# Between two layers: splitting the five later Silus of ScalarE into two and three

## The chip, the cores and the metric

The kernel runs on one core of a Trainium2 chip. The metric is the device time of one execution in microseconds; the figure of a kernel is the median of several executions. The five engines work in parallel, each through its own instructions in program order, and meet at semaphores: PE (TensorE, with its weight loads PEld), DVE (VectorE), ACT (ScalarE), POOL (GpSimd) and SP, which only issues DMAs.

## The reference

Two layers, each of the form `x = x + s * silu(g)` with `xn = layernorm(x)`; `s` comes from an attention-like part, `g` from a mixture of experts.

```python
x = L0_attn_x                                   # (4, 1024, 256): 4096 tokens
xn = _layernorm(x, axis=-1)
s = _L0_attn_ref(xn, ...)                       # windows of 64 tokens, 16 heads
g = _silu(_L0_ffn_ref(xn, ...))                 # 32 experts, one per token
x = x + s * g
xn = _layernorm(x, axis=-1)
s = _L1_attn_ref(xn, ...)                       # Fourier spectra, cumulative sum over tokens
g = _silu(_L1_ffn_ref(xn, ...))                 # 8 experts, two per token
x = x + s * g
```

The change lies between the layers: in `x = x + s * g` of the first, and in the layernorm, the transposition and the first spectra of the second.

## The kernel before

The 4096 tokens are 32 tiles of 128 rows; `X`, `XN` and `S` in SBUF hold x, the normalized x (later the first layer's mixture output, reloaded into the same place) and s. Between the layers the work goes by eight **quarters** of four tiles, numbered q = 0 to 7, with first tile g = 4q. For each quarter there are these steps, and the name of a step stands in a plan that each engine reads in order, doing its own part of it:

- `mix_load` (SP, L2545): the mixture's output is loaded into `XN`.
- `mix_silu` (ACT, L2213): Silu in place over 128x1024.
- `mix_mul` (DVE, L1591): `S = XN * S` over 128x1024.
- `mix_sum`: `X = X + S`, on DVE for quarters 0 and 1 (L1598), on POOL for 2 to 7 (L2370); SP then stores the quarter of `X` (L2560).
- `stats` (DVE, L1355 to L1360): mean and variance of the four tiles, and variance + eps; then ACT takes the square root (L2078).
- `norm`: DVE takes the reciprocal of the root (L1365), the shift (L1367), and normalizes two of the four tiles (L1371); ACT normalizes the other two (L2223); SP stores them (L2549).
- `turn`: PE transposes the quarter (L1037), ACT copies it from PSUM to `XT1` (L2085).
- `spectrum`: one of the second layer's spectra on PE (L1048). Its copy out of PSUM, `spectrum_out` (L2069), is put off until the plan next asks for it with `need`.
- `route1`: for every two quarters, router logits on PE (L1247), copied to `route1_rows` by ACT (L2237), and later `route1_turn`, their transposition (L1076) and copy (L2242). After the last of these DVE adds the router's bias (L1698) and starts the routing of the second layer.

The plan of this part is written out by hand in `combination()` inside `schedule0`. An item that is put off with a lag of 0 (`route1_out`) comes into the plan at the next `add`; one with the lag `LATER` comes only when `need` names it.

Silu and Sqrt are in different activation tables. Where an ACTIVATE needs another table than the one loaded, an ACT_TABLE_LOAD stands ahead of it on ACT; Copy and Identity need none of their own. Such a load has the line of the instruction that it serves (L2213 for Silu, L2078 for the root).

What each engine waits for at the places in question, in the words of the code:

```python
elif what == "mix_silu":                      # ACT: only for the load of its quarter
    w.wait_ge(x_in[q], 32)
if what == "stats":                           # ACT: the root waits for DVE's variance
    w.wait_ge(ln_var, nth)
def normalize(layer, g):                      # DVE: waits for the root on ACT
    w.wait_ge(ln_root, nth)
elif what == "route1_out":                    # ACT: waits for PE's router logits
    filled_by(use["route1", g])
elif what == "mix_mul":                       # DVE: waits for the Silu
    w.wait_ge(gated0, q + 1)
```

Of the kernel before, what the change touches and what calls it, by code (L numbers as in the profile page):

```python
# [132 lines left out]
QUARTERS = NT // 4  # L133
# [17 lines left out]
class Order:  # L151
# [10 lines left out]
    def need(self, item):  # L162
        for due, _, pending in list(self.late):
            if pending == item:
                self.settle(due)

    def add(self, what, *at):
        self.settle(self.clock)
        self.plan.append((what, *at))
# [31 lines left out]
LATER = STEPS * UT  # L201
SPECTRA_AHEAD = [(ch, n) for ch in range(AHEAD) for n in (KK, VV, QQ)]


def spectrum_bank(ch, n):
    return (3 * ch + (KK, VV, QQ).index(n)) % 2


def schedule0(banks):

    order = Order(banks)
    add, need = order.add, order.need
# [52 lines left out]
    def turn(layer, g, tiles=8):  # L265
        for t in range(g, g + tiles, 2):
            order.take(("turn", layer, t // 2), (4, 5)[(t // 2) % 2])
        add("turn", layer, g)
# [16 lines left out]
    def route1(g):  # L285
        order.product("route1", g, columns=0, then=[("route1_out", 0)])

    def route1_turn(g):
        need(("route1_out", g))
        order.product("route1_turn", g, columns=0, then=[("route1_turn_out", LATER)])  # L290
# [89 lines left out]
    def spectrum(ch, n, lag):  # L380
        order.product("spectrum", ch, n, bank=spectrum_bank(ch, n), columns=0, then=[("spectrum_out", lag)])

    def combination():
        add("load_wf")
        for q in range(QUARTERS):
            add("mix_load", q)
        for q in range(3):
            add("mix_silu", q)
        add("mix_mul", 0)
        add("mix_sum", 0)  # L390
        add("stats", 1, 0)
        add("norm", 1, 0)
        turn(1, 0, 4)
        spectrum(*SPECTRA_AHEAD[0], LATER)
        for q in range(3, QUARTERS):
            add("mix_silu", q)
        add("mix_mul", 1)
        add("mix_sum", 1)
        add("mix_mul", 2)
        add("mix_sum", 2)  # L400
        add("stats", 1, 4)
        add("mix_mul", 3)
        add("mix_sum", 3)
        add("stats", 1, 8)
        for q in range(1, QUARTERS):
            g = 4 * q
            if q % 2 == 0:
                need(("route1_turn_out", g - 8))
            add("norm", 1, g)
            if q + 3 < QUARTERS:  # L410
                add("mix_mul", q + 3)
                add("mix_sum", q + 3)
            need(("spectrum_out", *SPECTRA_AHEAD[q - 1]))
            turn(1, g, 4)
            if q % 2 == 0:
                route1_turn(g - 8)
            spectrum(*SPECTRA_AHEAD[q], LATER)
            if q % 2:
                route1(g - 4)
            if q + 2 < QUARTERS:  # L420
                add("stats", 1, g + 8)
        need(("spectrum_out", *SPECTRA_AHEAD[QUARTERS - 1]))
        route1_turn(4 * QUARTERS - 8)
        need(("route1_turn_out", 4 * QUARTERS - 8))
# [28 lines left out]
    assert next(ffn, None) is None  # L453
    order.settle(order.clock + STEPS * UT)
    combination()
    order.settle(order.clock + STEPS * UT)
    return order.plan
# [2216 lines left out]
```

## Time and profile before

| | |
|---|---|
| median of 3 runs | 1121.63 us (1120.66 to 1124.16) |
| the profiled execution | 1117.8 us, span of its instructions 1115.8 us |
| PE / DVE / ACT / POOL busy in the span | 92% / 62% / 48% / 37% |
| mean granted TensorE clock | 0.968 of full speed |

The profiled execution is one more execution beside the timed ones; its times below are microseconds from the start of its span. "Busy" of an engine is the share of the span in which it worked on an instruction. The chain of waits is followed back from the last instruction, at each step to what released it. The first layer ends on PE at about 420 us, the stretch between the layers ends at about 472 us, where DVE starts the routing of the second layer, and the second layer's experts run on PE from about 534 us to the end.

### The profile page before, as it was taken

How to read it: one execution, taken by the hardware profiler on the slowest of the kernel's cores; microseconds unless marked ns; L12 is line 12 of the kernel's file. 1: busy time of each engine (PE TensorE's matmuls, PEld its weight loads, DVE VectorE, ACT ScalarE, POOL GpSimd, SP SyncE). 2: the span in 40 equal slices, each digit the busy share in tenths (PEclk: the TensorE clock that was granted, in tenths of full speed). 3: DMA queues.
4: the chain of work that ended last, by engine and by line, in shares of the span. 5: the costliest groups of instructions: out<-in, count | busy, mean ns of one | idle time of the engine just before them, and what ended most of it. 6: DMA issues, size and time to landing. Idle time of an engine off the chain costs nothing.

```text
span 1115.8 us, 16806 instructions
## 1 busy us (share of the span) xinstructions
PE 1026.7 (92%) x6152; PEld 886.4 (79%) x6152; DVE 688.6 (62%) x1490; ACT 532.2 (48%) x1102; POOL 418.1 (37%) x391
## 2 busy tenths in 40 slices
PE   3867899999999994979999999999999999999994
PEld 2655788888888873668889998988888888888884
DVE  6796777777777767687846644474676100148753
ACT  3633754555545536733454545455353222356531
POOL 1056545554455452200243322332331345432273
PEclk9988999999999996987999999999999999999998
DMA  9932245445565428525497754544344679899961
GB/s 301 283 141 86 81 124 189 153 153 180 163 193 190 126 89 275 184 95 249 103 350 260 291 204 180 203 166 156 110 168 154 241 265 343 320 336 389 392 256 55
DMA packets 120402, 228.65 MB, mean 205 GB/s; under 512 B 14939, under 2 KB 103915, under 8 KB 115329
## 3 DMA queue, kind: packets, MB, share of 16 engines
q1 hardware_dynamic: 106448, 189.31, 48.7%
q0 software_dynamic: 13872, 38.27, 10.4%
q8 instruction: 49, 0.80, 0.3%
q14 instruction: 33, 0.26, 0.1%
HBM read 166.98 MB, written 62.79 MB: 206 GB/s over the span
## 4 chain that ended last, share of the span: by engine, by line
PE 74%; DVE 12%; ACT 4%; issue 3%; DMA 3%; POOL 2%; SPq 0%; POOLq 0%; DVEq 0%; ACTq 0%
PE PS L1314 21%; PE PS L1324 20%; PE PS L1213 6%; PE PS L1048 4%; PE PS L1098 3%; PE PS L1152 3%; PE PS L1223 2%; PE PS L1179 2%; PE PS L1107 2%; POOL table L2335 2%; PE PS L1165 2%; PE PS L1190 2%; DVE stats L1355 1%; PE PS L1300 1%; PE PS L1289 1%
## 5 line engine op out<-in xcount | busy, mean ns | idle before, releaser
L2292 ACT ACTIVATE hT<-PS,WE 128x256 f32<-128x256 f32 (+1 forms) x312 | 141.0, 454 | 255.2 <-PE PS L1314 240.1
L1314 PE MATMUL PS<-xgT,WE 128*128 128x256 f32 (+1 forms) x1248 | 253.3, 361 | 2.6 <-ACT hT L2292 1.8
L1324 PE MATMUL PS<-WE,hT 128*128 128x256 f32 x1104 | 244.6, 379 | 0.0
L1314 PEld LDWEIGHTS PS<-xgT,WE 128*128 128x128 f32 x1248 | 219.4, 190 | 29.4 <-ACT hT L2292 2.5
L1324 PEld LDWEIGHTS PS<-WE,hT 128*128 128x128 f32 x1104 | 207.4, 190 | 26.9
L1951 DVE TENSOR_TENSOR y<-PS,WE 128x512 f32<-128x512 f32 (+1 forms) x38 | 24.3, 640 | 206.9 <-PE PS L1324 201.7
L2410 POOL DMA_INDIRECT result<-y,result_of x53 | 53.8, 1016 | 175.8 <-DVE y L1951 168.6
L2398 POOL DMA_INDIRECT xg<-xn_dram,token_of x71 | 74.3, 1046 | 90.7 <-DVE result_of L1867 68.7
L1048 PE MATMUL PS<-XT,Wf 128*128 128x256 f32 x384 | 93.4, 399 | 3.3 <-ACT Z L2069 3.3
L1048 PEld LDWEIGHTS PS<-XT,Wf 128*128 128x128 f32 x384 | 75.1, 201 | 15.3 <-ACT Z L2069 4.9
L2351 POOL TENSOR_TENSOR prob<-prob,row_sum 128x512 f32<-128x512 f32 x56 | 58.6, 1046 | 59.8 <-DVE row_sum L1531 59.1
L1213 PE MATMUL PS<-rowsT,wgu 128*128 128x160 f32 x512 | 75.6, 301 | 0.0
L2344 POOL TENSOR_TENSOR sc<-sc,sc_max 128x512 f32<-128x512 f32 x56 | 58.5, 1045 | 42.7 <-DVE sc_max L1519 42.3
L1213 PEld LDWEIGHTS PS<-rowsT,wgu 128*128 128x128 f32 x512 | 71.9, 190 | 2.3 <-issue 1.4
L1098 PE MATMUL PS<-XT,qkv_w 128*128 128x256 f32 x256 | 64.6, 397 | 0.0
L1529 DVE TENSOR_REDUCE row_sum<-prob 128x8 f32<-128x512 f32 x64 | 43.5, 680 | 29.0 <-ACT prob L2160 26.0
L2386 POOL TENSOR_TENSOR MAG<-SQ 128x768 f32<-128x768 f32 x13 | 25.0, 1926 | 93.2 <-ACT SQ L2259 93.2
L1037 PE MATMUL PS<-const,XN 128*128 128x128 f32 x128 | 26.0, 353 | 35.9 <-DVE XN L1371 34.0
L2362 POOL DMA_INDIRECT mixed_dram<-y,row_token x40 | 39.7, 993 | 47.4 <-DVE y L1585 43.0
L2170 ACT ACTIVATE PT<-PS 128x512 f32<-128x512 f32 x64 | 38.3, 599 | 39.7 <-PE PS L1165 37.5
L1098 PEld LDWEIGHTS PS<-XT,qkv_w 128*128 128x128 f32 x256 | 48.0, 197 | 8.3 <-issue 1.1
L2335 POOL DMA_INDIRECT table<-XN,slot_put x32 | 32.4, 1012 | 58.0 <-DVE slot_put L1459 42.5
(280 smaller groups left out, 1711.9 us busy)
## 6 DMA issues: line engine op xcount, KB each, us to landing
WE<-in_experts SPq DMA_DIRECT2D x39, 2180.0 KB
wgu<-in_w_gate SPq DMA_DIRECT2D x32, 256.0 KB
wgu<-in_w_up SPq DMA_DIRECT2D x32, 256.0 KB
wdn<-in_w_down SPq DMA_DIRECT2D x32, 256.0 KB
result<-zeros SPq DMA_DIRECT2D x16, 512.0 KB
xs<-late_dram SPq DMA_DIRECT2D x16, 512.0 KB, 12.9
both<-result SPq DMA_DIRECT2D x16, 512.0 KB
table<-zeros POOLq DMA_DIRECT2D x1, 5160.0 KB, 31.2
```

Of the source, the lines that this page charges most:

```text
L1048: m = e.matmul(PS[:, u.bank, part * CH:(part + 1) * CH], Wf[:, n, k, part * P:(part + 1) * P], XT1[:, ch, k, :], start=k == 0, stop=k == K ...
L1098: m = e.matmul(PS[:, u.bank, c * UT:(c + 1) * UT], qkv_w[:, k, col:col + P], XT0[:, unit, k, :], start=k == 0, stop=k == KD - 1)
L1213: m = e.matmul(PS[:, u.bank + f, n * CAP:(n + 1) * CAP], wgu0[:, ex % 2, n, k, f * P:(f + 1) * P], rowsT[:, grp % 2, k, j * CAP:(j + 1) * ...
L1314: m = e.matmul(PS[:, FIRST_H_BANK + nth % HR, 0:rows], W1[n % WR][:, k, c * P:(c + 1) * P], xgT[:, n % 2, k, 0:rows], start=k == 0, stop=k ...
L1324: m = e.matmul(PS[:, u.bank, j * D:(j + 1) * D], hT[:, n % 2, c, j * P:(j + 1) * P], W2[n % WR][:, c, :], start=c == 0, stop=c == KF - 1)
L1529: e.tensor_reduce(row_sum[:, s % RR, :], prob[:, s % PR0, :, :], AX.X, ALU.add).then_inc(row_sum_done, 1)
L2292: e.activation(hT[:, n % 2, c, 0:rows], PS[:, FIRST_H_BANK + (KF * n + c) % HR, 0:rows], ACT.Gelu_apprx_tanh, bias=b1[n % WR][:, c:c + 1], ...
L2335: e.indirect_dma_start(out=table0, out_offset=bass.IndirectOffsetOnAxis(ap=slot_put[:, t:t + 1], axis=0), in_=XN[:, t, :], in_offset=None, ...
L2344: e.tensor_tensor(by_head, by_head, sc_max[:, s % SR, :].unsqueeze(2).to_broadcast([P, PAIRS, WIN]), ALU.subtract).then_inc(sc_sub_done, 1)
L2351: e.tensor_tensor(prob[:, s % PR0, :, :], prob[:, s % PR0, :, :], row_sum[:, s % RR, :].unsqueeze(2).to_broadcast([P, PAIRS, WIN]), ALU.mu ...
L2398: e.indirect_dma_start(out=xg[:, n % XR, j, :], out_offset=None, in_=xn_dram, in_offset=bass.IndirectOffsetOnAxis(ap=token_of[:, tile:tile ...
L2410: e.indirect_dma_start(out=result1, out_offset=bass.IndirectOffsetOnAxis(ap=result_of[:, tile:tile + 1], axis=0), in_=y1[:, n % YR, j, :], ...
```

## The change

The edit is in `combination()` alone. Before, the five Silus of quarters 3 to 7 follow each other on ACT, and the roots of quarters 1 and 2 follow them. Now the Silus of quarters 3 and 4 come first, then a table load, the root, the normalization, the transposition, the second spectrum and the first router logits of quarter 1, then a table load, the Silus of 5 to 7, a further table load and the roots of quarters 2 and 3. The first pass of the loop over quarters is written out ahead of it, so the loop starts at 2; `mix_mul` of quarter 4 and `stats` of quarter 3, which that pass held, stand before the loop too. No other work is added or removed.

```diff
         turn(1, 0, 4)
         spectrum(*SPECTRA_AHEAD[0], LATER)
-        for q in range(3, QUARTERS):
+        for q in range(3, 5):
             add("mix_silu", q)
         add("mix_mul", 1)
         add("mix_sum", 1)
         add("mix_mul", 2)
         add("mix_sum", 2)
         add("stats", 1, 4)
+        add("norm", 1, 4)
         add("mix_mul", 3)
         add("mix_sum", 3)
+        need(("spectrum_out", *SPECTRA_AHEAD[0]))
+        turn(1, 4, 4)
+        spectrum(*SPECTRA_AHEAD[1], LATER)
+        route1(0)
+        for q in range(5, QUARTERS):
+            add("mix_silu", q)
         add("stats", 1, 8)
-        for q in range(1, QUARTERS):
+        add("mix_mul", 4)
+        add("mix_sum", 4)
+        add("stats", 1, 12)
+        for q in range(2, QUARTERS):
             g = 4 * q
             if q % 2 == 0:
                 need(("route1_turn_out", g - 8))
```

In the changed kernel every line from L405 on has a number ten higher (the Silu, L2213, is L2223; the root, L2078, is L2088).

On ACT, from the copies of quarter 0's transposition to the root after the first router logits, before (XT_72 is `XT1`, route_rows is `route1_rows`):

```order
L2085 ACTIVATE XT_72<-PS 128x512 x2
L2213 ACT_TABLE_LOAD
L2213 ACTIVATE XN<-XN 128x4x256 x5
L2078 ACT_TABLE_LOAD
L2078 ACTIVATE rstd<-rstd 128x4 x2
L2223 ACTIVATE XN<-X,shift,rstd 128x256 x2
L2069 ACTIVATE Z<-PS,bf 128x256 x2
L2085 ACTIVATE XT_72<-PS 128x512 x2
L2237 ACTIVATE route_rows<-PS 128x256
L2078 ACTIVATE rstd<-rstd 128x4
```

and now, at the same place of ACT:

```order
L2223 ACTIVATE XN<-XN 128x4x256 x2
L2088 ACT_TABLE_LOAD
L2088 ACTIVATE rstd<-rstd 128x4
L2233 ACTIVATE XN<-X,shift,rstd 128x256 x2
L2079 ACTIVATE Z<-PS,bf 128x256 x2
L2095 ACTIVATE XT_72<-PS 128x512 x2
L2247 ACTIVATE route_rows<-PS 128x256
L2223 ACT_TABLE_LOAD
L2223 ACTIVATE XN<-XN 128x4x256 x3
L2088 ACT_TABLE_LOAD
L2088 ACTIVATE rstd<-rstd 128x4 x2
```

Three Silus have moved behind the copy of the router logits, with a table load ahead of them and another behind them; the roots of quarters 2 and 3 (the last row) follow these.

On DVE, from the end of quarter 1's statistics to the reciprocal of quarter 1's root, before (the rows left out are three more pairs of statistics):

```order
L1360 TENSOR_SCALAR rstd<-mean_var 128x4
L1591 TENSOR_TENSOR S<-XN,S 128x1024
L1355 BN_STATS stats<-X 128x6
L1357 BN_AGGR mean_var<-stats 128x2
...
L1360 TENSOR_SCALAR rstd<-mean_var 128x4
L1365 RECIPROCAL rstd<-rstd 128x4
```

and now, from the same row:

```order
L1370 TENSOR_SCALAR rstd<-mean_var 128x4
L1375 RECIPROCAL rstd<-rstd 128x4
L1377 SCALAR_TENSOR_TENSOR shift<-mean_var,rstd 128x4
L1381 TENSOR_SCALAR XN<-X,mean_var,rstd 128x256 x2
L1601 TENSOR_TENSOR S<-XN,S 128x1024
L1365 BN_STATS stats<-X 128x6
```

The normalization of quarter 1 has moved ahead of quarter 3's product and quarter 2's statistics; from quarter 4's product on, DVE's row of instructions is as before. PE's is as before throughout.

## Rows read from the trace of the kernel before

**Rows 1.** The page: the span of the profiled execution.
```profile
span 1115.8 us, 16806 instructions
```

**Rows 2.** Busy time by stretch: PE, PEld, DVE, ACT, POOL; granted clock; DMA share, GB/s.
```profile
418.00:472.00 54.00, 35.32 (x212) 25.71 (x209) 38.22 (x117) 39.05 (x78) 14.15 (x6) 0.84 0.71 237
440.00:441.00 1.00, 0.39 (x2) 0.24 (x2) 0.96 (x5) 0.73 (x2) 0.00 (x0) 0.50 0.82 275
445.00:446.00 1.00, 1.00 (x15) 0.49 (x17) 1.00 (x3) 0.00 (x0) 0.00 (x0) 1.00 0.62 209
```

**Rows 3.** The chain of waits between the layers: start, us, what.
```profile
433.46 4.84 ACT XN L2213 x5
...
471.91 0.44 DVE sc L1698
```

**Rows 4.** Timeline of DVE: start, us, instruction, idle before and its releaser.
```profile
435.62 1.21 DVE L1591 TENSOR_TENSOR S<-XN,S 128x1024 f32<-128x1024 f32 x1
...
439.00 0.29 DVE L1360 TENSOR_SCALAR rstd<-mean_var 128x4 f32<-128x4 f32 x1
439.86 0.18 DVE L1365 RECIPROCAL rstd<-rstd 128x4 f32<-128x4 f32 x1 [0.57 <-ACT rstd L2078]
...
440.80 1.22 DVE L1591 TENSOR_TENSOR S<-XN,S 128x1024 f32<-128x1024 f32 x1
...
444.39 0.17 DVE L1365 RECIPROCAL rstd<-rstd 128x4 f32<-128x4 f32 x1
...
457.97 0.16 DVE L1365 RECIPROCAL rstd<-rstd 128x4 f32<-128x4 f32 x1
```

**Rows 5.** Timeline of ACT between the layers.
```profile
428.44 0.20 ACT L2078 ACTIVATE rstd<-rstd 128x4 f32<-128x4 f32 x1 [0.77 <-DVE rstd L1360]
...
432.17 1.28 ACT L2213 ACT_TABLE_LOAD   x1
433.46 4.84 ACT L2213 ACTIVATE XN<-XN 128x1024 f32<-128x1024 f32 x5
438.33 1.28 ACT L2078 ACT_TABLE_LOAD   x1
439.62 0.30 ACT L2078 ACTIVATE rstd<-rstd 128x4 f32<-128x4 f32 x2
...
446.54 0.38 ACT L2237 ACTIVATE route_rows<-PS 128x256 f32<-128x256 f32 x1 [3.21 <-PE PS L1247]
446.82 0.20 ACT L2078 ACTIVATE rstd<-rstd 128x4 f32<-128x4 f32 x1
```

**Rows 6.** Timeline of PE between the layers.
```profile
431.40 3.47 PE L1048 MATMUL PS<-XT,Wf 128*128 128x256 f32 x8
440.62 2.08 PE L1037 MATMUL PS<-const,XN 128*128 128x128 f32 x8 [5.75 <-DVE XN L1371]
442.49 2.99 PE L1048 MATMUL PS<-XT,Wf 128*128 128x256 f32 x8
445.40 1.07 PE L1247 MATMUL PS<-XT,router 128*32 128x256 f32 x16
...
451.25 1.89 PE L1048 MATMUL PS<-XT,Wf 128*128 128x256 f32 x8
...
458.80 1.26 PE L1037 MATMUL PS<-const,XN 128*128 128x128 f32 x8 [0.58 <-DVE XN L1371]
```

**Rows 7.** Timeline of POOL: the sum of quarter 3.
```profile
436.91 2.35 POOL L2370 TENSOR_TENSOR X<-X,S 128x1024 f32<-128x1024 f32 x1 [1.23 <-DVE S L1591]
```

**Rows 8.** The chain of waits again: one spectrum at full clock, and four later PE pieces.
```profile
465.13 1.73 PE PS L1048 x8
...
502.49 3.66 PE PS L1278 x16
506.15 3.51 PE PS L1048 x8
...
520.50 3.66 PE PS L1278 x16
524.16 8.23 PE PS L1048 x32
```

## The prediction, made before the changed kernel was timed

> **What bounds the kernel now.** I read the stretch between the layers first, since all that moves lies in it. The profiled execution spans 1115.8 us [rows 1]. From 418 to 472 us no engine is full: PE is busy for 35.32 of 54 us, DVE for 38.22, ACT for 39.05 [rows 2]. So a wait decides, and the chain of waits says which: it runs through ACT's five Silus at 433.46 (4.84 us) and ends with DVE's first routing step at 471.91 [rows 3]. Between these two the chain is DVE nearly throughout. The timeline of DVE shows why: after the products and statistics of its plan it waits 0.57 us for quarter 1's root, takes the reciprocal at 439.86, and then never stands still; the reciprocal of quarter 2 is at 444.39, that of quarter 5 at 457.97 [rows 4]. That is 13.58 us for three quarters, 4.53 each, with no idle time noted. The reader should see two things: the Silus cost DVE only 0.57 us here, and DVE's work after 439.86 is a fixed sum that can't be shortened by getting a root earlier.
>
> ACT and PE have room in it. ACT stands idle for 3.21 us before it can copy the first router logits at 446.54 [rows 5]; PE stands idle for 5.75 us before quarter 1's turn at 440.62, and again 0.58 us before quarter 5's at 458.80, released by DVE [rows 6].
>
> **The change part by part.** Work is moved, and two table loads are added, nothing else. I follow ACT, and then ask when DVE gets the roots.
>
> Step 1, quarter 1's root comes earlier. Five Silus take 4.84 us, 0.97 each [rows 5]. Two now end at 433.46 + 1.94 = 435.40. From the end of the Silus (438.30) to the root (439.62) were 1.32 us, and to the reciprocal on DVE another 0.24 [rows 4, 5]. Now that is 435.40 + 1.32 + 0.24 = 436.96, which is 2.90 us earlier. DVE has quarter 1's statistics behind it where its next product began, at 435.62 [rows 4], so it now waits 1.34 us instead of 0.57. The product of quarter 3 and the statistics of quarter 2, which lay ahead of the reciprocal, now follow it: same work, other order. DVE alone would reach quarter 2's reciprocal at 444.39 - 0.57 + 1.34 = 445.16. So the first half of the change costs DVE 0.77 us, whatever PE gains. POOL's sum of quarter 3 takes 2.35 us [rows 7]. It would start when quarter 3's product is done: the four steps of the normalization take 440.80 - 439.86 = 0.94, the product 1.21, so about 439.1, and it ends at 441.5. Quarter 3's statistics come after quarter 4's product, at about 442.8; POOL holds nobody up.
>
> Step 2, the router logits stand ahead of the second three Silus. This is the term that decides. ACT works in order, and its row is now: normalize, copy, copy router logits, load, three Silus, load, roots. The logits need quarter 1's turn, a spectrum and the router product on PE. From the reciprocal (439.86) to the copy (446.54) it took 6.68 us [rows 4, 5], of which PE's three pieces are 5.85 (440.62 to 445.40 + 1.07) [rows 6]. Taken as it is: 436.96 + 6.68 = 443.64. The three Silus had nothing to wait for; ACT idles meanwhile.
>
> Step 3, from the copy to quarter 2's root: copy 0.38, load up to the first Silu 1.29 (432.17 to 433.46), three Silus 2.90, load and root 1.32, reciprocal 0.24 [rows 4, 5]. Together 6.13, so the reciprocal is at 449.77 instead of 444.39: **5.38 us later**. DVE, ready at 445.16, stands still for 4.6 us. Behind the waiting reciprocal are quarter 5's product, quarter 4's statistics and all the rest of the stretch. POOL and PE wait for these.
>
> Step 4, is any of it given back before 471.91? After that reciprocal DVE has the same instructions as before, at 4.53 us a quarter without a pause, so it can't catch up. Root 3 is taken together with root 2; the later roots had been on time and keep their distance to DVE. PE restarts after a longer pause, but what it has to do for a quarter is a turn and a spectrum, 1.26 + 1.89 us, and half a router product, below 4.53 [rows 6]; it is on time again by quarter 5, where it had 0.58 us to spare already. SP's store of quarter 1's `XN` moves ahead of a store of `X`; nobody in this stretch waits for either. After 471.91 the chain goes on through DVE's routing, so I let the whole 5.38 us pass to the end.
>
> The sum: 0.77 + 4.61 = 5.38. On the profiled execution 1117.8 + 5.4 = 1123.2. That execution lay 3.8 us under the median of the shown runs, so on the median 1121.63 + 5.4 = **1127.0**.
>
> The uncertain size is PE's 5.85 us, because the clock changes in it. The granted clock was 0.50 (the 1.2 GHz level) at 440 us, after PE's pause, and 1.00 (2.4 GHz) at 445 us, with PE at work from 440.62 [rows 2, 6]. The same eight matmuls of a spectrum took 3.47 at the low level, 2.99 across the change, 1.89 at the high one [rows 6]. PE's pause ahead of quarter 1's turn is now 5.75 - 2.90 = 2.85 us. If the clock doesn't fall in that, the spectrum is 1.1 shorter and the turn (2.08) about 1.0: the delay is 5.4 - 2.1 = 3.3. If all of it ran at the low level, the spectrum is 0.5 longer and the router product (1.07) about 1.1: 5.4 + 1.6 = 7.0. I take it as measured, since the nearest row is the very same three pieces after a pause.
>
> What speaks against the change in the rows is that the loads cost 1.28 us each with the next instruction right behind: the Silu starts 0.01 us after its load ended, the root likewise [rows 5]. The Trainium skill ("ScalarE: Activation LUTs", What ACT_TABLE_LOAD costs, and the rules for kernel authors) has about 1.28 us for a load and about 1.38 for a drain with it, and says to do all of one set before switching. The load agrees with this trace, the drain doesn't show in it. By the page the two added switches would cost 2.76 us more, an estimate of 1129.8.
>
> **The rivals.**
> (A) PE sets the pace after the gap. PE, not DVE, was nearly full from 442.49 on, with turn 2 taken up at about 446.47; now it would be at 449.77 + 0.76 = 450.53. If that sets the end, the delay is 4.1: 1125.7. Against it: the pause of 0.58 at 458.80, released by DVE.
> (B) PE's restart isn't absorbed. Turn and spectrum at the low clock, 2.08 + 3.47 against 1.26 + 1.89, are 2.4 us longer. If a root on ACT is kept back by it: 5.4 + 2.4 = 7.8, so 1129.4. Against it is the slack that step 4 finds.
> (C) A switch costs more than its load where ACT comes out of other work. The one pause seen behind a load is 0.77 us, put down to DVE [rows 5]; were it the switch's, the two added ones make 1.5: 1128.5. The page named above stands behind this; the rows give it little.
> (D) Not slower, by one mechanism: the clock in the routing part. On the chain at 502.49, 506.15, 520.50 and 524.16 PE pieces take 3.66, 3.51, 3.66 and 8.23 us [rows 8], mostly at the low level; a spectrum in the same chain takes 1.73, twice the speed of the 3.51. At the high level they would be about 1.8, 1.8, 1.8 and 1.3 shorter, 6.7 in all. A shifted start can move them against the clock's steps. If all four gain, 5.4 - 6.7 = -1.3, so 1120.3; from 5.4 us of such gain on the change isn't slower. It can as well lose, and it has no reason to side with the change.
> (E) The change doesn't do what it says, say that the three Silus don't wait behind the logits. Then only step 1 is left, +0.8: 1122.4. The order of ACT's instructions excludes it but for an error of mine in reading `route1_out`.
>
> **How the numbers follow.** Forecast 0.66, A 0.12, B 0.08, C 0.04, D 0.07, E 0.03. The likeliest gives 1127.0. The range takes the bounds of the clock term, +3.3 and +7.0, and 1.3 us more at either side for the medians, whose three runs lie 3.5 apart: 1123.6 to 1130.0. That also holds A, B and C. A measurement of this kernel can tell about 0.3% (3.4 us) from no change. Slower by more: nearly all of the forecast and of B and C, most of A: 0.80. Within: the low end of the clock term, some of A, E and half of D: 0.15. Faster: the rest of D, and what I overlook: 0.05.
>
> **What would show it.** In the changed profile: quarter 1's reciprocal near 437.0 after a wait of 1.3 us; the logits' copy near 443.6 with ACT idle for some 3 us before; right behind it a load, three Silus of 2.9 us, a load; quarter 2's reciprocal near 449.8 after a DVE wait of 4.6 us for the root; after it 4.53 us a quarter again; the first routing step near 477.3. Two more table loads on ACT between the layers. I am wrong if that DVE wait is under 2 us, if DVE's quarters after it are shorter than 4.5 us, or if the routing step is late by 5.4 and the end isn't.

## The result

| | before | changed |
|---|---|---|
| median of 10 runs | 1121.47 us (1120.15 to 1124.16) | 1126.45 us (1123.34 to 1131.93) |
| profiled execution, its span | 1117.8, 1115.8 us | 1123.34, 1121.4 us |
| mean granted TensorE clock | 0.968 | 0.967 |

The changed kernel takes 1.0042 times as long, 95% interval 1.0026 to 1.0059: 5.0 us more by the medians. The forecast was 1127.0 (5.4 us more, added to 1121.63, the median of the first three runs) with a range of 1123.6 to 1130.0. In microseconds the interval of the ratio goes from 2.9 to 6.6, so the medians can't tell 5.0 from 5.4; the rows below carry the account.

From the page of the changed kernel, the span and the busy times:

```profile
span 1121.4 us, 16808 instructions
PE 1028.4 (92%) x6152; PEld 887.5 (79%) x6152; DVE 688.3 (61%) x1490; ACT 536.7 (48%) x1104; POOL 418.7 (37%) x391
```

DVE is busy for 688.3 us and was for 688.6; ACT for 536.7 instead of 532.2, of which the two loads are 2.6. PE has 1.7 us more. None of this is on a full engine between the layers, so the time went into waits.

DVE's timeline in the changed kernel (lines are ten higher, L1375 is the reciprocal, L1601 the product); it answers to [rows 4]:

```profile
427.99 0.18 DVE L1375 RECIPROCAL rstd<-rstd 128x4 f32<-128x4 f32 x1 [0.27 <-ACT rstd L2088]
...
436.33 0.18 DVE L1375 RECIPROCAL rstd<-rstd 128x4 f32<-128x4 f32 x1 [1.32 <-ACT rstd L2088]
...
448.91 0.18 DVE L1375 RECIPROCAL rstd<-rstd 128x4 f32<-128x4 f32 x1 [4.39 <-ACT rstd L2088]
...
453.43 0.17 DVE L1375 RECIPROCAL rstd<-rstd 128x4 f32<-128x4 f32 x1
...
462.47 0.16 DVE L1375 RECIPROCAL rstd<-rstd 128x4 f32<-128x4 f32 x1
...
476.42 0.43 DVE L1708 TENSOR_TENSOR sc<-router_out,router_b 128x256 f32<-128x256 f32 x1 [7.53 <-ACT router_out L2252]
```

Two rows have a wait for the root: 1.32 us at quarter 1's reciprocal (436.33) and 4.39 at quarter 2's (448.91). Before, there was one, of 0.57, at quarter 1's. From quarter 2 to quarter 5 it is one reciprocal in 4.52 us and no wait, as before.

The two traces don't start this stretch at the same moment: quarter 0's reciprocal is at 428.68 before and at 427.99 here. I therefore measure from there. To DVE's first routing step it was 471.91 - 428.68 = 43.23 us, and is 476.42 - 427.99 = 48.43: **5.20 us more**. The spans differ by 5.6: 0.69 less ahead of this stretch, 5.20 in it, 1.1 more behind it (the last lines on why the prediction was right come back to these).

ACT's timeline shows what DVE waited for; it answers to [rows 5]:

```profile
431.48 1.28 ACT L2223 ACT_TABLE_LOAD   x1
432.78 2.00 ACT L2223 ACTIVATE XN<-XN 128x1024 f32<-128x1024 f32 x2
434.80 1.28 ACT L2088 ACT_TABLE_LOAD   x1
436.10 0.21 ACT L2088 ACTIVATE rstd<-rstd 128x4 f32<-128x4 f32 x1
...
442.71 0.38 ACT L2247 ACTIVATE route_rows<-PS 128x256 f32<-128x256 f32 x1 [2.91 <-PE PS L1257]
443.12 1.28 ACT L2223 ACT_TABLE_LOAD   x1
444.41 2.95 ACT L2223 ACTIVATE XN<-XN 128x1024 f32<-128x1024 f32 x3
447.38 1.28 ACT L2088 ACT_TABLE_LOAD   x1
448.67 0.30 ACT L2088 ACTIVATE rstd<-rstd 128x4 f32<-128x4 f32 x2
```

The reader should see the 2.91 us in which ACT stands idle for PE's router product, and right behind it, without a gap, the copy, a load, three Silus, a load and the roots. Those Silus needed nothing from PE. And PE, which answers to [rows 6]:

```profile
437.09 2.08 PE L1047 MATMUL PS<-const,XN 128*128 128x128 f32 x8 [2.93 <-DVE XN L1381]
438.96 2.68 PE L1058 MATMUL PS<-XT,Wf 128*128 128x256 f32 x8
441.58 1.07 PE L1257 MATMUL PS<-XT,router 128*32 128x256 f32 x16
449.66 2.08 PE L1047 MATMUL PS<-const,XN 128*128 128x128 f32 x8 [7.02 <-DVE XN L1381]
```

Quarter 1's turn starts after a pause of 2.93 us instead of 5.75, but quarter 2's after one of 7.02, where before it had none: the 2.8 us that PE was given at the first it lost more than twice over at the second.

The chain of waits in the changed kernel, with the same pieces as [rows 3] and [rows 8]; it now passes through PE's router product and the three Silus:

```profile
441.64 1.05 PE PS L1257 x16
...
445.37 1.99 ACT XN L2223 x2
447.38 1.28 ACT L2088
...
507.00 3.66 PE PS L1288 x16
510.66 3.51 PE PS L1058 x8
...
525.78 3.56 PE PS L1288 x16
529.33 8.69 PE PS L1058 x32
```

### The profile page after: what moved, and what is told of

Same layout as the page of the kernel before. It is cut to its first block, busy times and chain, and to the rows that moved or that the text cites. A ratio compares the mean times of both kernels' runs of the same rounds, so it can differ in the third digit from the quotient of the medians.

```text
span 1121.4 us, 16808 instructions
## 1 busy us (share of the span) xinstructions
PE 1028.4 (92%) x6152; PEld 887.5 (79%) x6152; DVE 688.3 (61%) x1490; ACT 536.7 (48%) x1104; POOL 418.7 (37%) x391
## 4 chain that ended last, share of the span: by engine, by line
PE 77%; DVE 10%; ACT 4%; issue 3%; POOL 2%; DMA 2%; SPq 0%; POOLq 0%; DVEq 0%; ACTq 0%
PE PS L1324 22%; PE PS L1334 21%; PE PS L1223 6%; PE PS L1058 4%; PE PS L1108 3%; PE PS L1162 3%; PE PS L1233 2%; PE PS L1189 2%; PE PS L1117 2%; POOL table L2345 2%; PE PS L1175 2%; PE PS L1200 2%; PE PS L1299 1%; PE PS L1310 1%; DVE stats L1365 1%
## 5 line engine op out<-in xcount | busy, mean ns | idle before, releaser
L1047 PEld LDWEIGHTS PS<-const,XN 128*128 128x128 f32 x128 | 19.5, 181 | 46.6 <-DVE XN L1381 23.2
```

Source lines behind the costliest of these rows:

```text
L1047: m = e.transpose(out_v[:, k, j * P:(j + 1) * P], XN[:, 2 * pair + j, k * P:(k + 1) * P], ident)
```

## The experiments

The theory is that of the forecast: the loss is DVE standing still for roots which ACT takes late because its three Silus stand behind the wait for the router logits. The rivals are that PE's pace sets the end (A), that the table switches cost more than their loads (C), and that DVE's new order matters little. All time differences below are over the kernel before, and "the stretch" is the time from quarter 0's reciprocal to DVE's first routing step, 43.23 us before and 48.43 changed. It is one execution each, but its parts repeat closely: from quarter 0's reciprocal to quarter 1's it is 11.18 us in the kernel before and in each of the three below that differ from it only behind that point. The medians scatter by 1 us or more. In the expectations of the first four kernels "stretch" is counted from the first load of the mixture's output, 53.46 and 58.66 us; I compare the differences.

**The three Silus ahead of the logits' copy.** Of the changed kernel:

```diff
-        route1(0)
         for q in range(5, QUARTERS):
             add("mix_silu", q)
+        route1(0)
         add("stats", 1, 8)
```

> The changed kernel with one edit: the three later Silus stand ahead of the copy of the router logits on ACT, not behind it. The stretch from the first load of the mixture's output to DVE's first routing step is 53.46 us in the kernel before and 58.66 in the changed one. Theory (ACT's three Silus wait behind the logits, and DVE's quarter 2 behind them): the Silus start right after quarter 1's copies (439.81), so in the time of the changed kernel's trace load, Silus, the logits' copy, load and root put quarter 2's reciprocal at 439.81 + 1.29 + 2.95 + 0.4 + 1.3 + 0.24 = 446.0 instead of 448.91: 2.9 us of the 5.2 are given back, stretch 55.7, median about 2.2 us over before (1123.7). Rival A (PE's pace sets the end): PE's first quarters are as before, so little is given back and the stretch stays over 57.5. Rival C (the table switches cost more than their loads): DVE still waits over 3 us at that reciprocal.

Measured: stretch 45.39, 2.16 us over before (2.2 expected), so 3.04 of the 5.20 are given back. Ratio to the kernel before 1.0009 (0.9994 to 1.0024), median 1122.49. DVE's wait at quarter 2's reciprocal fell from 4.39 to 1.34, in DVE's timeline:

```profile
446.49 0.18 DVE L1375 RECIPROCAL rstd<-rstd 128x4 f32<-128x4 f32 x1 [1.34 <-ACT rstd L2088]
```

The place of the Silus behind the wait for PE is thus worth 3 us, by a move on ACT alone. Of the 2.16 us that are left, 0.75 are the longer wait at quarter 1's reciprocal and 1.34 this one.

**The three Silus ahead of quarter 1's copies too.** Of the changed kernel, in place of its lines between quarter 3's `mix_sum` and the loop:

```diff
+        for q in range(5, QUARTERS):
+            add("mix_silu", q)
+        add("stats", 1, 8)
         need(("spectrum_out", *SPECTRA_AHEAD[0]))
         turn(1, 4, 4)
         spectrum(*SPECTRA_AHEAD[1], LATER)
-        route1(0)
-        for q in range(5, QUARTERS):
-            add("mix_silu", q)
-        add("stats", 1, 8)
         add("mix_mul", 4)
         add("mix_sum", 4)
+        route1(0)
         add("stats", 1, 12)
```

> The changed kernel with the three later Silus and quarter 2's root moved right behind quarter 1's normalization on ACT, ahead of the copies of its turn and of the logits; both added table loads stay. Theory: quarter 2's root is then ready (443.4 in the time of the changed kernel's trace) before DVE comes to it (444.4), so DVE waits only at quarter 1's reciprocal, 1.3 us instead of 0.57: stretch 53.46 + 0.77 = 54.2, median 1122.3. Rival A (PE sets the pace): quarter 1's copies come some 5 us later for PE than in the changed kernel, so the stretch is longer than 56. Rival C (switches cost more than their loads): the stretch is 55.5 or more, since root and copies come later.

Measured: quarter 2's reciprocal waits for nothing, as the theory said. But the stretch is 44.98, 1.75 us over before and not 0.77; median 1122.08, ratio 1.0009 (0.9993 to 1.0025). The missing 1 us lies at the end, where DVE's last root comes late, as DVE's timeline shows:

```profile
469.39 0.18 DVE L1375 RECIPROCAL rstd<-rstd 128x4 f32<-128x4 f32 x1 [2.15 <-ACT rstd L2088]
```

and where PE's waits are for ACT's tiles and no longer for DVE:

```profile
462.22 0.33 PE L1047 MATMUL PS<-const,XN 128*128 128x128 f32 x1 [0.50 <-ACT XN L2233]
```

The last root waited 1.12 us before and waits 2.15 here. So a part of rival A is true: PE and ACT had less than 1.75 us of room. This was the first sign of what the forecast had sized wrongly.

**Two more switches.** Of the kernel before; the two added ACTIVATEs are of one column and their results are used by nobody:

```diff
+                if layer and g == 4:
+                    e.activation(rstd[:, NT - 2:NT - 1], C["ones"][:, 0:1], ACT.Sqrt)
+                    e.activation(rstd[:, NT - 1:NT], C["ones"][:, 0:1], ACT.Silu)
                 w.wait_ge(ln_var, nth)
                 e.activation(rstd[:, g:g + n], rstd[:, g:g + n], ACT.Sqrt).then_inc(ln_root, 1)
```

> The kernel before with two ACTIVATEs of one column (a Sqrt and a Silu) between the five Silus and quarter 1's root, which force a load for Sqrt, a load for Silu and then the load that was there: two more switches on the path that DVE waits for. Theory: a switch costs its load alone, so two loads of 1.29 and two small ACTIVATEs of about 0.2 each delay quarter 1's reciprocal by 2.9 to 3.0 us, all of it exposed: stretch 56.4, median 1124.5. Rival C, by the pause of 0.77 us seen once behind a load: 1.5 more, stretch 57.9. By the price that the Trainium skill gives for a switch (about 2.66 us with its drain, ScalarE: Activation LUTs, What ACT_TABLE_LOAD costs) it would be 2 x 2.66 + 0.4 = 5.7, stretch 59.2.

Measured: stretch 46.21, 2.98 over before. Median 1123.88, ratio 1.0032 (1.0017 to 1.0046). ACT's timeline has the loads 1.50 us apart, a load of 1.28 and a small ACTIVATE between each two:

```profile
437.39 1.28 ACT L2078 ACT_TABLE_LOAD   x1
...
438.89 1.28 ACT L2079 ACT_TABLE_LOAD   x1
...
440.39 1.28 ACT L2081 ACT_TABLE_LOAD   x1
```

and DVE's, the reciprocal behind them, after a wait of 3.57 us instead of 0.57:

```profile
441.93 0.18 DVE L1365 RECIPROCAL rstd<-rstd 128x4 f32<-128x4 f32 x1 [3.57 <-ACT rstd L2081]
```

Rival C falls: a switch costs its load here, and nothing behind it. The estimate of 5.7 us by the figure of the Trainium skill ("ScalarE: Activation LUTs", What ACT_TABLE_LOAD costs) is not what was measured, and the measurement decides.

**DVE's new order alone.** Of the changed kernel:

```diff
-        for q in range(3, 5):
+        for q in range(3, QUARTERS):
             add("mix_silu", q)
...
-        for q in range(5, QUARTERS):
-            add("mix_silu", q)
```

> The changed kernel with all five later Silus together again, as before the change, so no table load is added; what is left is DVE's new order (normalization of quarter 1 ahead of quarter 3's product and quarter 2's statistics). Theory: DVE now waits from the end of quarter 1's statistics to the root that comes behind five Silus, 4.2 us instead of 0.57, and nothing of that is given back: stretch 53.46 + 3.7 = 57.1, median 1125.1; quarter 2's reciprocal then doesn't wait. Rival (DVE's order matters little because PE or ACT sets the pace): the stretch stays within 1 us of 53.5.

Measured: stretch 46.79, 3.56 over before; DVE's wait at quarter 1's reciprocal is 4.15 us. Median 1126.04, ratio 1.0044 (1.0029 to 1.0060). DVE's timeline, the reciprocals of quarters 1 and 2:

```profile
440.97 0.18 DVE L1373 RECIPROCAL rstd<-rstd 128x4 f32<-128x4 f32 x1 [4.15 <-ACT rstd L2086]
449.09 0.17 DVE L1373 RECIPROCAL rstd<-rstd 128x4 f32<-128x4 f32 x1
```

As expected: a wait that DVE takes before its other work is a wait paid in full. The change's first half is this order, kept cheap (0.75 us) by the earlier root.

**DVE's old order with the split.** Of the changed kernel:

```diff
-        add("norm", 1, 4)
         add("mix_mul", 3)
         add("mix_sum", 3)
+        add("stats", 1, 8)
+        add("norm", 1, 4)
...
         for q in range(5, QUARTERS):
             add("mix_silu", q)
-        add("stats", 1, 8)
         add("mix_mul", 4)
```

> The changed kernel with DVE's old order: quarter 3's product and quarter 2's statistics stand ahead of quarter 1's normalization again, and so quarter 2's root is taken with quarter 1's, ahead of the three Silus, which still stand behind the logits' copy. From quarter 0's reciprocal to DVE's first routing step it is 43.23 us in the kernel before and 48.43 in the changed one. Theory (DVE stands still until ACT has waited for the logits and done what is behind them; which instruction waits doesn't matter): neither reciprocal waits, but quarter 5's product now waits about 3.7 us for its Silu, and quarter 3's reciprocal for its root; in all 3.2 us over before, 46.4, median 1124.7. Rival (the loss came from the two roots behind the loads, not from the Silus): about 43, no product waits.

Measured: stretch 49.60, 6.37 over before and not 3.2. Median 1128.63, ratio 1.0066 (1.0041 to 1.0091). The first part is as expected: quarter 5's product waits 3.98 us for its Silu, and quarter 3's reciprocal is 23.60 us after quarter 0's, 3.36 more than before. Then a further 3.0 us are lost, at two roots late on ACT. DVE's timeline:

```profile
450.38 1.22 DVE L1601 TENSOR_TENSOR S<-XN,S 128x1024 f32<-128x1024 f32 x1 [3.98 <-ACT XN L2223]
...
463.73 0.18 DVE L1375 RECIPROCAL rstd<-rstd 128x4 f32<-128x4 f32 x1 [0.65 <-ACT rstd L2088]
...
471.41 0.18 DVE L1375 RECIPROCAL rstd<-rstd 128x4 f32<-128x4 f32 x1 [3.38 <-ACT rstd L2088]
```

**One Silu late.** Of the kernel before:

```diff
-        for q in range(3, QUARTERS):
+        for q in range(3, QUARTERS - 1):
             add("mix_silu", q)
...
             spectrum(*SPECTRA_AHEAD[q], LATER)
+            if q == 1:
+                add("mix_silu", QUARTERS - 1)
             if q % 2:
                 route1(g - 4)
```

> The kernel before with a smaller split: Silus of quarters 3 to 6 together, that of quarter 7 alone behind the copies of quarter 1's turn and ahead of the logits' copy, with its two table loads; DVE's order as before. Quarter 7's product is some 15 us away, so nobody waits for it. Theory: quarter 1's root comes 0.97 us earlier and DVE's wait of 0.57 us goes; DVE is the bound, so the gain is 0.57: from quarter 0's reciprocal to the first routing step 42.7 instead of 43.23, median 1121.0, which a timing can't tell from no change. Rival (PE's lag at the tail, as with the Silus ahead of the turn): ACT's part of quarter 2 and with it PE's turn come about 1 us later, DVE's last root is late, and it is 43.2 or more.

Measured: stretch 43.67, 0.44 over before, so the rival has it. Quarter 2's reciprocal did come 0.68 us sooner after quarter 0's, but the last root waits 2.02. Median 1121.61, ratio 0.9990 (0.9969 to 1.0010), no difference that can be told.

**Four tiles from DVE to ACT.** Of the kernel before (the wait for a normalized group is fitted to it):

```diff
-        return t % 8 < 5 if layer == 0 else t % 4 < 2
+        return t % 8 < 5 if layer == 0 else t % 4 < (1 if 8 <= t < 24 else 2)
...
-        wait_normalized(w, layer, g + 1 if layer else g + 4)
+        wait_normalized(w, layer, (g if 8 <= g < 24 else g + 1) if layer else g + 4)
```

> The kernel before with one of DVE's two normalized tiles of each of quarters 2 to 5 given to ACT (three on ACT, one on DVE); no Silu is moved. Theory (between the layers DVE's work is a fixed sum that sets the end): each quarter is 0.33 us shorter on DVE, 4.53 becomes 4.20, four quarters 1.3; the turn of quarter 5 waits for ACT's third tile, so 1.0 to 1.3 is left: 42.1 from quarter 0's reciprocal to the first routing step instead of 43.23, median 1120.4. Rival A (PE or ACT sets the pace): the reciprocals stay 4.5 us apart or the last root gets later, and it is 43.2 or more.

Measured: DVE's quarters are 4.20 us, as expected, and quarter 5's reciprocal is 28.31 us after quarter 0's instead of 29.29. Yet the stretch is 43.78, 0.55 over before. Median 1122.39, ratio 0.9998 (0.9986 to 1.0009). The gain went into the last root. DVE's timeline:

```profile
456.95 0.17 DVE L1365 RECIPROCAL rstd<-rstd 128x4 f32<-128x4 f32 x1
...
463.87 0.18 DVE L1365 RECIPROCAL rstd<-rstd 128x4 f32<-128x4 f32 x1 [2.97 <-ACT rstd L2078]
```

**Both together.** On the kernel before, the edits of the last two.

> The one late Silu and the tiles given to ACT together, on the kernel before. Theory: both gains add up, 0.57 + 1.1: 41.6 from quarter 0's reciprocal to the first routing step, median 1119.9. Rival: ACT, which now has the late Silu, two loads and four more tiles, falls behind in quarters 2 and 3, DVE's roots wait there, and it is over 42.5.

Measured: stretch 46.58, 3.35 over before, median 1126.12, ratio 1.0040 (1.0024 to 1.0056). The rival again, and by more than either edit alone.

**What these misses have in common.** The five kernels whose stretch came out longer than expected are the Silus ahead of the copies, the split with the old DVE order, and the last three. In each of them the logits' copies on ACT follow each other by 7.67 us at the end (8.60 where ACT has three tiles a quarter), whatever DVE does. Two copies are two quarters apart, and DVE takes 9.05 for two. So there are two branches, and the later one sets the stretch. DVE's branch is quarter 5's reciprocal + 13.95 us. The branch of PE and ACT is the second logits' copy + 2 x 7.67 + 1.39. (The 13.95 are 4.89 to the third logits' copy and then the same 7.67 + 1.39, so the last two quarters go at the pace of PE and ACT in either branch.) All in us after quarter 0's reciprocal:

| kernel | DVE's branch | PE's and ACT's | measured |
|---|---|---|---|
| before | 43.24 | 42.27 | 43.23 |
| changed | 48.43 | 47.37 | 48.43 |
| Silus ahead of the logits' copy | 45.40 | 44.03 | 45.39 |
| Silus ahead of the copies | 43.96 | 44.98 | 44.98 |
| two more switches | 46.21 | 45.41 | 46.21 |
| five Silus together | 46.79 | 45.42 | 46.79 |
| split, old DVE order | 47.32 | 49.59 | 49.60 |
| one Silu late | 42.78 | 43.67 | 43.67 |
| tiles to ACT (one pair 8.60) | 42.26 | 43.78 | 43.78 |
| both (one pair 8.60) | 43.38 | 46.58 | 46.58 |

The two constants were read off these traces, so the table is an account and no proof. What it says can be tested, though: in the 7.67 us, ACT copies the logits, and only then takes its root and its two tiles, for which PE waits. PE's timeline in the kernel before has the wait, in the turn of quarter 6:

```profile
463.87 0.33 PE L1037 MATMUL PS<-const,XN 128*128 128x128 f32 x1 [0.50 <-ACT XN L2223]
```

and ACT's, at the same time, the copy, the root and the tiles:

```profile
462.86 0.38 ACT L2237 ACTIVATE route_rows<-PS 128x256 f32<-128x256 f32 x1 [1.57 <-PE PS L1247]
463.13 0.20 ACT L2078 ACTIVATE rstd<-rstd 128x4 f32<-128x4 f32 x1
463.23 1.08 ACT L2223 ACTIVATE XN<-X,shift,rstd 128x256 f32<-128x256 f32 x2
```

**The logits' copy behind ACT's tiles.** Of the kernel before:

```diff
-        order.product("route1", g, columns=0, then=[("route1_out", 0)])
+        order.product("route1", g, columns=0, then=[("route1_out", LATER)])
...
             add("norm", 1, g)
+            if q % 2 == 0:
+                need(("route1_out", g - 8))
```

> The kernel before with one edit: ACT copies the router logits of two quarters behind its own part of the next quarter's normalization, not ahead of it (no Silu, load, DVE or PE instruction is moved). What the earlier traces suggest: from quarter 0's reciprocal to DVE's first routing step the time is the later of two branches. DVE's: quarter 5's reciprocal + 13.95 us (43.23 before, 48.43 changed). PE's and ACT's: the second logits' copy + 2 x 7.67 + 1.39 (42.3 before, 47.4 changed); it wins with the Silus ahead of the turn, with the old DVE order, with one late Silu and with the tiles on ACT. The 7.67 us hold a wait of PE for ACT's tiles, which stand behind the copy. Theory: with the copy behind them that wait (1.3 us a pair of quarters) goes, the last pair takes 6.5 us, and since DVE's branch ends with such a pair too, it is 1.1 us shorter: 42.1 instead of 43.23, median 1120.6. Rival (the 13.95 us are DVE's and PE's own work): it stays at 43.2.

Measured: stretch 42.20, 1.03 less than before (1.1 expected). From the third copy to the fourth it is 6.27 us, in ACT's timeline:

```profile
464.13 0.37 ACT L2239 ACTIVATE route_rows<-PS 128x256 f32<-128x256 f32 x1
...
470.40 0.38 ACT L2239 ACTIVATE route_rows<-PS 128x256 f32<-128x256 f32 x1 [0.19 <-PE PS L1249]
```

and in DVE's the last root's wait is gone:

```profile
462.95 0.17 DVE L1367 RECIPROCAL rstd<-rstd 128x4 f32<-128x4 f32 x1
```

Median 1119.02, ratio 0.9988 (0.9973 to 1.0004): the time doesn't prove a gain by itself, the rows do for the stretch.

**The same with four tiles on ACT.**

> The same edit with the four tiles of quarters 2 to 5 given to ACT. Alone, those tiles made DVE's quarters 4.20 us long instead of 4.53, and the end came 0.55 us later all the same, by the branch of PE and ACT. Theory: with the copy out of that branch's way the DVE gain of 1.0 us to quarter 5 is left, and both add up: 41.1 from quarter 0's reciprocal to the first routing step, median 1119.6. Rival (PE's and ACT's branch is still the later one, since ACT has three tiles a quarter): 42 or more.

Measured: stretch 41.56, 1.67 less than before (2.1 expected). Median 1117.72, ratio 0.9967 (0.9951 to 0.9983), so this one is faster than before, and so than the changed kernel. The tiles, which alone made the stretch longer, now shorten it by 0.64.

**All three edits.**

> The kernel before with the logits' copy behind ACT's tiles, the four tiles given to ACT and the Silu of quarter 7 alone, late. The last took 0.68 us from quarter 2's reciprocal when it was tried alone, but delayed ACT in front of the logits' copy. Theory: if ACT has room now, 0.6 more than without it, 40.5, median 1119.0. Rival (the two loads and the Silu, 3.6 us, keep ACT's part of quarter 2 and PE's turn back): no gain over 41.1, or a loss, with DVE waiting for quarter 3's root or a later one.

Measured: stretch 41.02, 2.21 less than before (2.7 expected). Median 1117.78, ratio 0.9966 (0.9954 to 0.9979). The late Silu, a loss of 0.44 by itself, gains 0.54 here. Its time can't be told from that of the kernel without it. Both ratios are below what the stretch explains (0.9985 and 0.9980), and both intervals end just short of that (0.9983 and 0.9979); what the rest comes from is not shown.

**The changed kernel with the later copy.** The same two edits on the changed kernel; the copy then leaves its place ahead of the three Silus.

> The changed kernel with the logits' copy put behind ACT's part of the next normalization, which takes the three Silus out from behind it: ACT goes from quarter 1's copies straight to load, Silus, load and roots. Theory: quarter 2's reciprocal is 17.5 us after quarter 0's (15.71 before, 20.92 changed, 17.89 with the Silus ahead of the copy), and the last pair of quarters is 1.1 us shorter: 17.5 + 13.58 + 12.85 = 43.9 to the first routing step, median 1122.3. Rival (PE's clock and late restart cost, not ACT's order): over 46.

Measured: stretch 44.11, 0.88 over before (0.7 expected), 4.32 of the 5.20 given back. Median 1121.04, ratio 0.9992 (0.9977 to 1.0007). DVE's wait at quarter 2's reciprocal is 1.08 us.

## Why the prediction was right, and where not

Step 1 held. With the 0.69 us by which this trace is early, quarter 1's reciprocal was put at 436.96 and is at 437.02. DVE waits 1.32 us (1.34 forecast).

Step 2, the term that decides, was 0.3 us too large. The logits' copy came 442.71 - 436.33 = 6.38 us after the reciprocal, 6.68 in the forecast. The piece that differs is the spectrum, which took 2.68 us instead of 2.99. The turn ran at 2.08 as before, so PE's pause of 2.93 us was not short enough to keep the high level. The granted clock shows it: it had risen at the end of the spectrum ahead of the pause (0.57 on average in 432 to 434), stood at the high level through the pause, and fell as the turn began at 437.09. Busy time of PE by stretch, granted clock, DMA share, GB/s:

```profile
434.00:436.00 2.00, 0.16 (x1) 1.00 0.98 327
436.00:438.00 2.00, 0.91 (x4) 0.79 0.76 251
```

The forecast's low bound, 3.3 us, was the case that the clock doesn't fall in this pause. It fell. And the clock behind it, from the rows by stretches, as in [rows 2]:

```profile
440.00:441.00 1.00, 1.00 (x5) 0.85 (x4) 0.93 (x5) 0.00 (x0) 0.92 (x1) 0.72 0.29 101
450.00:451.00 1.00, 1.00 (x6) 1.00 (x6) 1.00 (x2) 1.00 (x3) 0.00 (x0) 0.50 0.00 0
455.00:456.00 1.00, 1.00 (x10) 0.97 (x9) 0.97 (x3) 1.00 (x4) 0.35 (x1) 1.00 1.02 328
```

It is 0.72 on average in 440 to 441: the step up to 2.4 GHz falls into that microsecond, with PE at work since 437.09. Before, it was still 0.50 at 443 to 444 and 0.65 in 444 to 445, with PE at work since 440.62. Counted from the turn, the step came sooner here, and so the spectrum is 0.3 us shorter. At 450, after the pause of 7 us, it is at the low level again (1.2 GHz, 0.50), and at 455 back at the high one.

Step 3 was forecast at 6.13 us and took 448.91 - 442.71 = 6.20. Together the second reciprocal is 5.21 us late, with 5.38 forecast; DVE stood still for 4.39, with 4.6 forecast.

Step 4 had the right outcome on a margin that it sized wrongly, and on a reading of the rows that doesn't hold to the end of the stretch. The forecast has the chain of waits as DVE's nearly throughout, and DVE as never standing still after 439.86. In the kernel before, that is so up to 458.66. From there to the first routing step, for 13 us, the chain of waits is PE's and ACT's:

```profile
458.80 1.26 PE PS L1037 x8
...
470.53 0.38 ACT route_rows L2237
```

and DVE's timeline has two waits in it:

```profile
463.36 0.18 DVE L1365 RECIPROCAL rstd<-rstd 128x4 f32<-128x4 f32 x1 [1.12 <-ACT rstd L2078]
...
471.91 0.42 DVE L1698 TENSOR_TENSOR sc<-router_out,router_b 128x256 f32<-128x256 f32 x1 [7.52 <-ACT router_out L2242]
```

So DVE's work is no fixed sum up to 471.91. The forecast still came out, because the delay had passed from DVE to PE by then, at quarter 5's turn (PE waits 0.67 us there for DVE, 0.58 before), and what follows took as long as before. All of the 5.21 passed to the first routing step (5.20). But the text took the slack of PE and ACT from a pause of 0.58 us on PE and from the sum of PE's work per quarter, 1.26 + 1.89 below 4.53. The slack that counts was 43.24 - 42.27 = 0.97 us before, and 1.06 changed. It is so small because PE's work isn't the whole loop: PE waits in it for ACT's two tiles behind the logits' copy. That is rival A (and B with it), and it was priced for the changed kernel only. There it lost by 1.06 us. Its price, 4.1 us, is what its branch comes to (47.37 - 43.23 = 4.14), but by chance: the forecast counted PE's later start at quarter 2 alone, while the branch came 5.10 us later and had 0.97 us of slack. In five of the kernels that I built after that it won, and each time my expectation was 1 to 5 us too good.

Rival C is refuted by the two more switches, E by ACT's row of instructions. D, the clock in the routing part, did not turn the result, but it shows in the rows with the other sign. The four pieces of [rows 8] took 3.66, 3.51, 3.66 and 8.23 us and now 3.66, 3.51, 3.56 and 8.69. Between the second and the third the chain of waits has one more piece of PE, before

```profile
509.66 1.76 PE PS L1278 x16
```

and in the changed kernel

```profile
514.16 2.52 PE PS L1288 x16
```

At its start the granted clock was 0.73 before (509 to 510) and 1.00 from 510 on; now it was 0.50 (514 to 515) and 0.68 (515 to 516). These three differences, 0.76 - 0.10 + 0.46, are the 1.1 us that the changed execution lost behind the stretch. One execution of each doesn't show that they belong to the change: in the twelve kernels of the experiments the time behind the stretch is from 1.0 us less to 2.9 us more than before, and doesn't follow the stretch.

The whole: 5.0 us by the medians, 5.2 in the stretch, 5.4 forecast. The mechanism and the sum for the stretch were right. That the medians agree with it to 0.4 us is partly luck, with an interval of 2.9 to 6.6 and parts outside the stretch that differ by more than 0.4 us between the profiled executions.

## What to carry to other kernels

Where an engine works in order and meets a wait for another engine, look at what stands behind the wait and needs nothing of it: here three Silus and two roots, 6 us of ACT, stood behind a copy that waited 2.9 us for PE, and DVE paid 4.4 us for it. Splitting a batch to make its first consumer early only helps if that consumer is not the engine whose work is already gap-free: DVE could have won 0.57 us at the most. And before giving a bound engine less to do, size the second branch; with only 1 us between them, taking 1 us of work from DVE made the stretch longer, until the other branch's wait was moved.

## What the runs showed of the hardware

A change of the activation table cost its load and nothing more: 1.28 us, with the next ACTIVATE 0.01 to 0.02 us behind it wherever that one waited for nothing; two added switches with two ACTIVATEs of one column cost 2.98 us.

A pause of PE of only 2.93 us cost the high clock: the turn behind it took 2.08 us at the low level, as it did after pauses of 5.75 and 7.02 us; with the clock at the high level it took 1.04 to 1.26. The length of the pause alone doesn't say what it costs. With the Silus ahead of the logits' copy and in the changed kernel with the later copy, PE paused 3.86 and 3.58 us ahead of quarter 2's turn, and the turn still took only 1.56 and 1.35 us; the clock fell only towards its end (1.00, then 0.62 in 448 to 449; 1.00, then 0.76 in 449 to 450), and the spectrum that followed took 3.20 and 3.11 us instead of 1.89.
